# The last 56 tiles of an edge loop as phases of 24, 24 and 8 tiles, with additions inside the softmax steps

## The reference

```
h = layernorm(x) @ W                                   # 4 heads x 64
scores = leaky_relu(e_s[edge_src] + e_d[edge_dst], 0.2)
ex = exp(scores - segment_max(scores, edge_dst)[edge_dst])
alpha = ex / max(segment_sum(ex, edge_dst)[edge_dst], 1e-9)
agg = segment_sum(alpha * h[edge_src], edge_dst)       # 2500 x 256
x = x + relu(agg)
x = x + experts(layernorm(x))                          # top 2 of 8, 256 -> 512 -> 256, gelu
```

## Time and profile before

| | us |
|---|---|
| device time, median of 3 runs | 1388.14 |
| lowest and highest | 1386.94, 1390.61 |
| profiled execution, first to last instruction (span) | 1249.1 |
| median less span | 139.0 |
| edge loop, from the first gather to the first instruction of the node stage | 78.6 to 953.8 |

### The profile page before, as it was taken

The page is one execution under the profiler, slowest core; times in us unless marked ns, Lnnn a source line. Parts: engine busy times, 40 slices in busy tenths (PEclk is TensorE's granted clock), DMA queues, the critical chain, the costliest instruction groups (busy, mean ns, idle before and its releaser), DMA issues.

```text
span 1249.1 us, 11021 instructions
## 1 busy us (share of the span) xinstructions
PE 661.5 (53%) x2666; PEld 524.6 (42%) x2666; DVE 726.1 (58%) x1781; ACT 419.7 (34%) x1058; POOL 784.9 (63%) x835
## 2 busy tenths in 40 slices
PE   0630343455335643465435643365447579999990
PEld 0520232244223432344324432244336558888880
DVE  6611476558665775558655775558677853333325
ACT  3550243144323443144423443144421532222210
POOL 5577777777777777777777777777710025555540
PEclk9975657787678766777677776776777579999995
DMA  8564434344444434444344444443491212222217
GB/s 281 177 119 108 110 106 109 109 111 110 107 110 110 110 107 108 109 111 110 107 111 110 111 107 109 109 111 106 118 357 44 84 34 69 76 72 72 68 59 254
DMA packets 79451, 143.95 MB, mean 115 GB/s; under 512 B 22337, under 2 KB 50467, under 8 KB 79267
## 3 DMA queue, kind: packets, MB, share of 16 engines
q0 software_dynamic: 39664, 110.31, 31.9%
q1 hardware_dynamic: 37147, 30.44, 8.0%
q10 hardware_dynamic: 2584, 2.56, 0.6%
HBM read 126.48 MB, written 17.40 MB: 115 GB/s over the span
## 4 chain that ended last, share of the span: by engine, by line
POOL 50%; PE 19%; issue 18%; DVE 6%; DMA 2%; PEld 1%; ACT 1%; PEldq 1%; DVEq 0%; POOLq 0%
POOL ring L529 49%; PE psum L731 7%; PE psum L745 7%; PE psum L592 1%; POOL ring L501 1%; PEld psum L641 1%; PEldq L643 1%; PE psum L719 1%; PE psum L683 1%; DVE acc L1479 1%; DVE acc L1480 1%; ACT ring L882 1%; PE psum L674 1%; DMA ring<-in_dst,ring 1%; DMA h_tab<-ring 1%
## 5 line engine op out<-in xcount | busy, mean ns | idle before, releaser
L529 POOL DMA_INDIRECT ring<-h_tab,srcP x664 | 630.8, 950 | 204.6 <-issue 201.9
L641 PE MATMUL psum<-ring,shared 128*128 128x260 f32 x1328 | 387.0, 448 | 450.5 <-DVE acc L1118 391.9
L641 PEld LDWEIGHTS psum<-ring,shared 128*128 128x128 f32 x1328 | 284.1, 222 | 540.2 <-DVE acc L1118 407.4
L826 ACT ACTIVATE shared<-iota_f,Dcol 128x128 f32<-128x128 f32 x664 | 202.0, 386 | 29.6 <-PEq L643 29.5
L1205 DVE TENSOR_TENSOR ring<-ring,psum 128x2048 f32<-128x2048 f32 x83 | 189.8, 2287 | 2.8
L844 ACT ACTIVATE Ex<-Z 128x128 f32<-128x128 f32 x21 | 6.5, 309 | 516.8 <-DVE Z L1172 516.8
L1118 DVE TENSOR_TENSOR acc<-acc,psum 128x260 f32 x332 | 140.0, 422 | 59.7 <-PEq L643 24.2
L1140 DVE STREAM_TRANSPOSE TB<-ring 128x128 f32<-128x128 f32 x21 | 8.5, 403 | 226.4 <-DMA ring<-h_tab,srcP 226.3
L540 POOL DMA_INDIRECT ring<-z_tab,ring x54 | 52.5, 972 | 116.4 <-DVEq L1418 100.3
L549 POOL DMA_INDIRECT ys_tab<-shared,ring x54 | 53.9, 998 | 85.5 <-DVE shared L1438 77.2
L928 ACT ACTIVATE RS_all<-psum,tail_consts 128x256 f32<-128x256 f32 x108 | 45.2, 470 | 158.0 <-PE psum L731 158.0
(11 more groups left out here) (293 smaller groups left out, 620.5 us busy)
## 6 DMA issues: line engine op xcount, KB each, us to landing
ring<-h_tab,srcP POOLq DMA_INDIRECT x664, 2.8
ring<-in_L_ffn_W SPq DMA_DIRECT2D x16, 512.0 KB, 11.0
h_tab<-ring SPq DMA_DIRECT2D x10, 260.0 KB, 2.6
ring<-in_x SPq DMA_DIRECT2D x1, 2432.0 KB
z_tab<-ring SPq DMA_DIRECT2D x2, 1024.0 KB, 4.4
ring<-ys_tab SPq DMA_DIRECT2D x4, 512.0 KB, 9.0
ring<-ys_tab ACTq DMA_DIRECT2D x4, 512.0 KB, 9.6
out<-acc SPq DMA_DIRECT2D x4, 512.0 KB
```

Source lines behind the costliest of these rows:

```text
L529: pool.indirect_dma_start(out=ring[:, t % RING, :], out_offset=None, in_=h_tab, in_offset=bass.IndirectOffsetOnAxis(ap=srcP[:, t:t + 1], a ...
L641: pe.matmul(sums[G_at % NSUM][:, 0:MW], dst_oh[:, n % OHB, 2 * g + r, :], ring[:, t % RING, :], start=(r == 0), stop=(r == 1))
L826: last = act.activation(dst_oh[:, n % OHB, k, :], iota_f[:, :], ACT.Square, scale=-1.0, bias=Dcol[:, t:t + 1])
```

## The change

The last 56 tiles, before one phase of 32 (phase 19) and one of 24 (phase 20), become phases 19, 20 and 21 of 24, 24 and 8 tiles, that is batches 76 to 78, 79 to 81, and 82. The batches themselves don't change, nor does what POOL gathers and in which order. There is one softmax step more. In a phase of fewer than 32 tiles `weights` copies the logits into `top` first, in two pieces where the ring wraps, and then transposes from there. The two last `weights` steps take an argument `between`: the number of a batch whose flush is run in the middle of the step. On ACT the one-hots of batch 79 come behind the exponential of phase 20, and those of batch 82 behind that of phase 21. SP has eight more small loads before the loop and one `load_chain` and `load_X` more in it. SP's waits for batches 75 and 79 keep their numbers.

```
     PH = 32
-    NPH = (NT + PH - 1) // PH
+    BT = 8
+    FULL = NT // PH - 1
+    MID = (NT - BT - FULL * PH) // 2
+    TILES = [PH] * FULL + [MID, MID, BT]
+    NPH = len(TILES)
+    FIRST = [sum(TILES[:f]) for f in range(NPH)]
...
-            rs_parts = rs_tab[0:NPH * PH, :].rearrange("(f t) (i r) -> i t f r", t=PH, i=SUB)
+            rs_parts = rs_tab[0:(FULL + 1) * PH, :].rearrange("(f t) (i r) -> i t f r", t=PH, i=SUB)
             for i in range(SUB):
-                sp.dma_start(rs_part[i * PH:(i + 1) * PH, :, :], rs_parts[i]).then_inc(rs_in, 16)
+                sp.dma_start(rs_part[i * PH:(i + 1) * PH, 0:FULL + 1, :], rs_parts[i]).then_inc(rs_in, 16)
+            for f in range(FULL + 1, NPH):
+                rs_late = rs_tab[FIRST[f]:FIRST[f] + PH, :].rearrange("t (i r) -> i t r", i=SUB)
+                for i in range(SUB):
+                    sp.dma_start(rs_part[i * PH:(i + 1) * PH, f, :], rs_late[i]).then_inc(rs_in, 16)
...
-            sp.wait_ge(batch_done, (NPH - 2) * PB)
+            sp.wait_ge(batch_done, FULL * PB)
...
-            sp.wait_ge(batch_done, (NPH - 1) * PB)
+            sp.wait_ge(batch_done, (FULL + 1) * PB)
...
-                    .then_inc(gathered[t // PH % len(gathered)], 16)
+                    .then_inc(gathered[phase_of(t) % len(gathered)], 16)
...
-            for f in range(NPH - 1):
+            for f in range(FULL):
                 n = f * PB
                 batch(n)
                 batch(n + 1)
                 batch(n + 2)
-                if f < NPH - 2:
-                    factor(f + 1)
+                factor(f + 1)
                 batch(n + 3)
-            factor(NPH - 1).then_inc(fac_in, 1)
-            for n in range((NPH - 1) * PB, NBAT):
-                batch(n)
+            for f in range(FULL, NPH):
+                for n in range(FIRST[f] // BT, (FIRST[f] + TILES[f]) // BT):
+                    batch(n)
+                if f + 1 < NPH:
+                    factor(f + 1).then_inc(fac_in, 1)
...
-            last = (NPH - 1) * PB
-            for n in range(last - 2, last + 1):
-                one_hots(n)
-            exponents(NPH - 1)
-            for n in range(last + 1, NBAT):
-                one_hots(n)
+            last = FULL * PB
+            one_hots(last + 2)
+            lay_seeds(FULL + 2)
+            exponents(FULL + 1)
+            one_hots(last + 3)
+            one_hots(last + 4)
+            one_hots(last + 5)
+            exponents(FULL + 2)
+            one_hots(last + 6)
...
-            def weights(f):
-
-                rs, rs_back, at = RS_all[:, f, 0:P], RS_all[:, f, 1:P + 1][:, ::-1], f * PH % RING
-                tiles = min(PH, NT - f * PH)
+            def weights(f, between=None):
+
+                rs, rs_back, at = RS_all[:, f, 0:P], RS_all[:, f, 1:P + 1][:, ::-1], FIRST[f] % RING
+                tiles = TILES[f]
+                parts = tiles * SUB
                 v.wait_ge(gathered[f % len(gathered)], 16 * (PH * (f // len(gathered)) + tiles))
                 es, top = TB[:, 0, :], TB[:, 1, :]
-                c.link(v.transpose(es.rearrange("p (h t) -> p h t", h=H),
-                                   ring[:, at:at + PH, HF:MW].rearrange("p t h -> p h t")))
+                if tiles == PH:
+                    c.link(v.transpose(es.rearrange("p (h t) -> p h t", h=H),
+                                       ring[:, at:at + PH, HF:MW].rearrange("p t h -> p h t")))
+                else:
+                    here = min(tiles, RING - at)
+                    by_head = top.rearrange("p (h t) -> p h t", h=H)
+                    last = v.tensor_copy(by_head[:, :, 0:here],
+                                         ring[:, at:at + here, HF:MW].rearrange("p t h -> p h t"))
+                    if here < tiles:
+                        last = v.tensor_copy(by_head[:, :, here:tiles],
+                                             ring[:, 0:tiles - here, HF:MW].rearrange("p t h -> p h t"))
+                    c.link(last)
+                    c.link(v.transpose(es, top))
...
+                if parts < P:
+                    v.memset(D_row[0:KH, parts:parts + 1], -BIG)
...
+                if between is not None:
+                    flush(between)
...
-            last = (NPH - 1) * PB
+            last = FULL * PB
+            weigh(last)
             flush(last - 2)
+            weigh(last + 1)
             flush(last - 1)
-            weights(NPH - 1)
-            factor(NPH - 1)
-            turn(NPH - 1)
-            weigh(last)
+            rescale(FULL)
+            gates(FULL + 1)
+            weigh(last + 2)
+            flush(last)
+            weights(FULL + 1, last + 1)
+            factor(FULL + 1)
+            turn(FULL + 1)
+            weigh(last + 3)
+            flush(last + 2)
             v.wait_ge(fac_in, 1)
-            rescale(NPH - 1)
-            for n in range(last + 1, NBAT):
-                weigh(n)
-                flush(n - 1)
-            flush(NBAT - 1)
+            rescale(FULL + 1)
+            gates(FULL + 2)
+            weigh(last + 4)
+            flush(last + 3)
+            weigh(last + 5)
+            weights(FULL + 2, last + 4)
+            factor(FULL + 2)
+            turn(FULL + 2)
+            weigh(last + 6)
+            flush(last + 5)
+            v.wait_ge(fac_in, 2)
+            rescale(FULL + 2)
+            flush(last + 6)
```

More of the change, by code:

```diff
@@ L67, in gat_moe_kernel @@
     KINDS = 3
-    BT = 8
     GB = BT // 2
@@ L71, in gat_moe_kernel @@
     PB = PH // BT
-    assert NT % BT == 0 and CHUNKS * P == E and RING % PH == 0 and H * PH == P
+    assert FULL * PB + 7 == NBAT and MID == 3 * BT
+    assert FIRST[-1] + BT == NT and BT < MID < PH and MID % BT == 0 and FIRST[-1] + PH <= NPH * PH and CHUNKS * P == E and RING % PH == 0 and H * PH == P
     MW = HF + H
@@ L237, in gat_moe_kernel @@
         n_blk, n_incl, n_excl = late(NE), late(NE), late(NE)
-        assert (NPH - 1) * PH % RING == 0 and used[0] <= PH * MW
+        assert (FULL + 1) * PH % RING == 0 and used[0] <= PH * MW
         used[0] = PH * MW
@@ L352, in numbers, with phase_of @@
                 skip_runtime_bounds_check_because="counts of a path that is bounded by its construction")[1]
+        def phase_of(t):
+            return max(f for f in range(NPH) if FIRST[f] <= t)
         NCONST = 9
@@ L401, in load_chain @@
                     sp.wait_ge(gates_made, f - 1)
-                first = f * PH * SUB
+                first = FIRST[f] * SUB
                 sp.dma_start(goes[f % 2][:, 0:P], chain_tab[0, first:first + P].partition_broadcast(PH))\
@@ L847, in exponents @@
                     act.activation(fm[:, :], old[:, :], ACT.Exp).then_inc(fac_made, 1)
-            act.wait_ge(rs_in, 16 * SUB)
+            act.wait_ge(rs_in, 16 * SUB * (NPH - FULL))
             act.activation(RS_all[:, :, 0:P].rearrange("p f (h r) -> p f h r", h=H),
@@ L858, in _ @@
             exponents(0)
-            for f in range(NPH - 2):
+            for f in range(FULL):
                 n = f * PB
@@ L1109, in _ @@
             c.link(v.tensor_scalar(blk_i[:, :], beta_pairs, float(NB - 1), None, ALU.min))
-            v.tensor_copy(d_first[:, :], rows[:, 1, 0:NPH * PH].rearrange("a (f t) -> a f t", t=PH)[:, :, 0])\
+            for f in range(FULL + 1, NPH):
+                last = v.tensor_copy(d_first[:, f:f + 1], rows[:, 1, FIRST[f]:FIRST[f] + 1])
+            c.link(last)
+            v.tensor_copy(d_first[:, 0:FULL + 1],
+                          rows[:, 1, 0:(FULL + 1) * PH].rearrange("a (f t) -> a f t", t=PH)[:, :, 0])\
              .then_inc(rows_read, 1)
@@ L1188, in rescale @@
             def rescale(f):
-                blk = numbers(mybir.EngineType.DVE, blk_i, f * PH // 2, 1, 0, NB - 1)[0]
+                blk = numbers(mybir.EngineType.DVE, blk_i, FIRST[f] // 2, 1, 0, NB - 1)[0]
                 v.tensor_scalar(fac[:, :], soft[:, 0:H], 1.0, None, ALU.add).then_inc(fac_used, 1)
@@ L1198, in weigh @@
             def weigh(n):
-                f, t0 = n // PB, n * BT
-                at, of = t0 % RING, t0 % PH
-                if n % PB == 0:
+                t0 = n * BT
+                f = phase_of(t0)
+                at, of = t0 % RING, t0 - FIRST[f]
+                if of == 0:
                     v.wait_ge(turned_w, f + 1)
@@ L1238, in _ @@
                 flush(n)
[L1239 to L1240 removed]
+                weights(f + 1)
                 weigh(n + 3)
[L1242 to L1243 removed]
+                factor(f + 1)
                 flush(n + 1)
[L1245 to L1247 removed]
+                turn(f + 1)
+            last = FULL * PB
+            weigh(last)
             flush(last - 2)
+            weigh(last + 1)
             flush(last - 1)
[L1250 to L1259 removed]
+            rescale(FULL)
[7 more added lines that the diff above has]
+            flush(last + 2)
+            v.wait_ge(fac_in, 1)
+            rescale(FULL + 1)
[11 more added lines that the diff above has]
+            flush(last + 6)
```

18 lines of the change are left out of this document (7 added, 11 removed).

## The result

The change makes the kernel slower: 1397.7 us (median of 4 runs, 1394.86 to 1401.84) against 1388.91 for the kernel before, timed beside it (4 runs, 1386.94 to 1390.61). The ratio of changed to before is 1.0072, with a 95% interval from 1.0056 to 1.0089, that is 8.8 us on 1397.7 against 1388.91. Forecast were +2.5 us, "no measurable change" as the likeliest, and 1395.6 as the upper end of the range.

The account below looks back on a forecast made before the run. From 883.14 to 953.84 DVE and PE were taken as the bound. Idle time of 16.0 us goes, 15.15 is added, the last wait grows by 0.9 to 4.0: +2.5 us, 1390.6, range 1385.0 to 1395.6.

Parts of the forecast that it names:

- Step 1: Softmax 19 needs tiles only up to 631, so it starts at 874.45 when DVE is free; 8.69 us of waiting go.
- Steps 2 to 6: From softmax 19 to the loop's end: copies, load overlap, longer softmax steps and slow batches, ending at 953.9 to 957.0.
- Step 3: Ahead of softmax 20: SP's loads start about 894.3 and meet some 14 gathers; tile 655 lands at 906.5, new wait 2.25 us.
- Step 4: Softmax 20 with flush 77 inside; PE, idle before, starts batch 79 slow, done at 928.5, and DVE waits 0.75 us.
- Steps 5 and 6: Softmax 21 takes 11.85 us; batch 82 follows some 8 us of idle PE; loop ends at 953.9, 955.8 or 957.0.
- wholly low: Batch 82 entirely at the low clock: last flush begins 6.98 us after the batch starts, loop ends at 957.0, 1391.3 us.
- half-low: Only the first half of batch 82 at the low clock: last flush begins about 953.6, loop ends at 955.8.
- A: Rival, chance 0.18: tile 655 lands undisturbed at 903.2, batches 79 and 82 run at full clock; 1385.2 us.
- B: Rival, chance 0.18: gathers queue behind the loads, tile 655 lands about 911.5, softmax 20 five us later; 1395.6 us.
- C: Rival, chance 0.08: PE's clock stays up into the node stage to about 981, at most 5.5 us faster; 1382.6 us.
- D: Rival, chance 0.08: third softmax overlaps badly, up to 3.2 us, 1393.8; under open questions, theory that the drain itself is late.
- N: Theory from the follow-ups, not the prediction: PE is held up whatever signals a batch done; without drains, within 1% of 1.

Follow-up runs that it names:

- e1: The kernel before, unedited, traced a second time: 1396.0 us against 1395.36 for the same kernel beside it, ratio 1.0003.
- e6: The changed kernel with a batch counted done by its last matmul and no drain behind it: 1256.87 us, 1.0041 of the kernel before.
- e10: The changed kernel, unedited, in a series at the fast pace: 1255.99 us, 1.0039 of the kernel before.
- e2: The changed kernel, unedited, run again beside the kernel before at the slow pace: 1404.93 us, ratio 1.0059.
- e3: The changed kernel with flushes 77 and 80 moved ahead of their softmax steps: 1404.36 us, 1.0069 of the kernel before.
- e4: The kernel before with flush 79 moved into the last softmax step: 1396.14 us, 1.0001 of the kernel before.
- e13: The changed kernel with SP's loads of x, w1 and w2 held until batch 78: 1253.08 us against 1251.02 for the kernel before, 1.0012.
- e17: The kernel before with a batch counted done by its last matmul and no drain behind it, a repeat: 1.001 of the kernel before.

## Why the prediction was wrong, step by step

**The basis.** The step that failed is "1388.14 - 1249.1 = 139.0", which I added to the sum as time around the span. It lies in the loop: 1395.0 us of span in e1, 1397.23 by the clock. The page had no time of its own, but 139 us of launch around the span was a claim, and I put no rival against it.

**Step 1, "This takes away 8.69".** True of the trace that I read (e6 and e10 start softmax 19 at 874.6 and 875.4), and not of the runs that were timed. In those, the tiles are long there (25 us in e1), DVE waits for PE's drain, and the gain is nought: no wait for tiles stands ahead of softmax 19 in e1, and the changed kernel has none to take away. So the ledger is without its largest credit, 8.69 us.

**Steps 2 to 6, what lies behind softmax 19.** From `weigh(75)` to the node stage I had 883.5 to 956.3 (953.84 + 2.5), that is 72.8 us or 10.8 more than before. Without the 2.25 us of step 3, which the slow pace doesn't have (the loads start behind the last gather there, at 1046 to 1052), it is 8.6 more. Measured: 69.9, 69.3 and 69.6 (the changed kernel, e2, e3) against 61.5 and 61.2 (e1, e4), 8.2 more on average. These steps were right in sum. At the fast pace e6, e10 and e13 take 74.2, 72.4 and 69.5, the last one without the loads ahead of the last gather.

- *Step 3*, SP's loads from 894.3 and a wait of 2.25 ahead of softmax 20: loads from 894.29 (e6) and 897.37 (e10); waits of 4.26 and 1.30. Right in kind. That e10's wait is near 2.25 is in part luck: the tile is used at 907.83 and not 906.5, and DVE itself comes at 906.5 and not 904.25, among other things because it waits 1.39 us for batch 75, which the ledger didn't have.
- *Step 4*, batch 79 starts slow: 5.69 us in e6, against 3.77 for the next (5.30 in e10, 6.51 in e13). DVE waits 0.47 for it at flush 79 in e13 and not at all in e6, against 0.75. Right in kind, a little too dear.
- *Steps 5 and 6*, batch 82 behind an idle PE: 6.78 us in e6, nearly the "wholly low" case:

```profile
923.62 5.69 PE L653 MATMUL psum<-ring,shared 128*128 128x260 f32 x16 [2.92 <-DVE ring L1244]
929.88 3.77 PE L653 MATMUL psum<-ring,shared 128*128 128x260 f32 x16 [0.57 <-DVE ring L1244]
...
945.41 0.58 PE L642 MATMUL psum<-fm,oh_row 1*128 1x4 f32 x2 [5.16 <-DVE fm L1219]
948.71 6.78 PE L653 MATMUL psum<-ring,shared 128*128 128x260 f32 x16 [2.72 <-DVE ring L1244]
```

PE was idle but for two small matmuls before both, and both are slow. In the other traces of the same phases batch 82 takes 6.39 (e10), 5.64 (e13), 5.37 (the changed kernel) and 6.27 (e2), so it is low for a part that varies. I had taken a value between the half-low and the low case, and that is where these lie. By the rule that I had cited (the Trainium skill, "TensorE: Matmul & The Clock Gate", "HAM oscillation — how this bites in real kernels") batch 82 was to start at the low clock; all five traces agree with that, and only e6, with 6.78 us, comes near to a batch that is low throughout.

**A term that I didn't have.** The stretch from the node stage to the end was 295.3 us, and 295.2 to 295.9 in other traces with the old phases (298.3 in e17); with changed phases it is 296.8 to 297.4. PE shows where. In the kernel before, and in e10:

```profile
1018.73 7.07 PE L731 MATMUL psum<-ring 128*128 128x256 f32 x32
```

```profile
1021.75 8.74 PE L744 MATMUL psum<-ring 128*128 128x256 f32 x32
```

These are the first 32 matmuls of the stage behind the node stage, and what follows is late by their difference. The windows, by the columns of the earlier trace rows, show the clock in their first 4 us, before:

```profile
1018.00:1022.00 4.00, 3.77 (x20) 3.38 (x21) 0.99 (x2) 0.84 (x2) 2.83 (x3) 1.00 0.37 98
```

and in e10, with the 6 us ahead of them:

```profile
1015.00:1021.00 6.00, 2.59 (x9) 0.99 (x7) 2.43 (x4) 0.00 (x0) 4.48 (x6) 1.00 0.29 87
...
1021.00:1025.00 4.00, 3.77 (x12) 3.12 (x13) 1.00 (x2) 0.00 (x0) 2.79 (x3) 0.59 0.34 98
```

The granted clock is 1.00 in the one and 0.59 in the other, with the same work ahead of them, only 3 us later. It doesn't come up late in e10: it is at 1.00 from 1015 to 1021, where PE has 2.59 us of work in 6 (1.70 us in the 4 from 1014 on in the trace of before), falls just as the 32 matmuls begin, and is back from 1025 on. By the clock's own records it rises at 1014.0 in the trace of before and stays up, and rises at 1014.9 in e10 and is low from 1021.7 to 1025.1; the changed kernel and e13 have the same dip. The 32 take 7.07 us in six of seven traces of kernels with the old phases (8.69 in e17, which has the dip too), and 8.03 to 8.76 in all thirteen with new ones. That is 1.0 to 1.7 us, and it counts at either pace. Why the level falls once more is open; e17 shows that it isn't bound to the change.

**The sums.** Fast pace, e10 against the first trace of before: the first gather is issued 0.4 us later, then +2.6 up to the node stage (877.8 against 875.2 us from the first gather), then +2.1; in all 1254.2 - 1249.1 = 5.1, and 4.9 by the timed ratio. My +2.5 was the middle term, and the one behind it was missing from the sum. Slow pace: 8.2 up to the node stage and 1.8 behind it are 10.0; timed were 8.8 in the first series and 8.2 in the second (1395.36 x 0.0059). The 1 to 2 us between are not accounted for; the late drains ahead of the stretch differ by more than that from one trace to the next (405 to 448 us in all).

**The rivals.** A (no late gathers and a warm PE) did not come. B has the sign, but neither its mechanism nor its size came: tile 655 took 5.96 us (6.40 in e6) and not over 7.9, so it did not stand behind the backlog, and the loads cost about 3.4 us in all, at the fast pace only. The rule that I set beside it (the Trainium skill, "DMA: Bandwidth & Descriptors", "Queues, rings and completion order") had the two queues take turns, and the 5.96 us are in line with it. C did not come: the clock fell in the node stage as before (it is at the low level from 956.8 to 1014.9 in e10, from 956.0 to 1014.0 in the trace of before). D did not come as a cost of flushes that overlap badly (e3, e4). What came stood in no rival: the gain of step 1 missing whole.

**What stays open.** What holds the drain up at the slow pace, and why a series runs at one pace or the other. The late drains belong to the time in which POOL issues gathers, but that is a coincidence in time and not shown as the cause. The gathers themselves are no slower: POOL's issues take 953 ns in e1 and 950 in the first trace, and their queue is busy for 28.5% of 1395.0 us and 31.9% of 1249.1, which is 398 us in both. That DVE's instructions come late too, ahead of any batch, speaks against D as the whole answer; N was not tested at the slow pace. Whether counting `batch_done` by the last matmul cures it was not seen, since no such kernel ran at the slow pace. That the third softmax step is the whole cost there rests on e3, on the timelines and on the ledger, not on a run with two steps.

## What to carry to other kernels

Compare the span of a profile with the times of the runs before anything is read from it. Where they differ by much more than the 1.8 to 2.2 us that lay outside the span in the runs here, as the 139 us did here, the trace may show another execution than the one that is to be improved, and each wait in it has to be found again in a second trace. A wait that a change is to remove must be there in the timed runs. Here it was not, and what the change paid for its removal, a further softmax step at the end of the loop, was left as cost.

At the end of a loop, look whether bulk loads for the next stage meet gathers that someone still waits for. At the fast pace they did, and one number in one wait gave back about 3.4 of 4.9 us; at the slow pace they didn't meet.

## What the runs showed of the hardware

One and the same kernel ran whole series at about 1390 us and others at about 1251, one of each on the same chip. Why is open. At the slow pace some 45 of 83 drains behind a batch of matmuls end late by 405 to 448 us together, all for batches that are done while POOL still issues gathers; DVE's single instructions come late too (216.6 us for 21 softmax steps against 171.4). The same bytes then move over a longer span (103 GB/s against 115). At the fast pace no drain is late, and replacing it by a count on the last matmul is worth nothing (1.0007, 1.0005, 1.0002, 1.001). A gather of 128 rows that alone landed 2.84 us after the start of its issue took 5.96 and 6.40 us until its use while loads of 8 MB ran beside it (e10, e6). And the clock granted to PE can fall back for 3.4 us just as a dense stretch of matmuls begins: 32 of them then take 8.03 to 8.76 us and not 7.07.
